# Router weights spread over the rows by DMA instead of by matmuls, in a gated cross-attention and mixture-of-experts block

## The reference, cut to what matters

```python
x = x + tanh(g_xattn) * xattn(layernorm(x), ctx)      # (4, 256, 256): both sides rounded to fp8 blocks, then x @ ctx.T
x = x + tanh(g_ffn) * ffn(layernorm(x))
def ffn(x):                                           # 1024 tokens of 256; 8 experts of 176 rows, top 4; shared of 704
    probs = softmax(x @ gate_w.T)
    comb = top4(probs), divided by their sum, 0 elsewhere         # (tokens, 8)
    y_e = (silu(x @ wg_e.T) * (x @ wu_e.T)) @ wd_e.T
    sh = (silu(x @ swg.T) * (x @ swu.T)) @ swd.T
    return sum_e comb_e * y_e + sigmoid(x @ shared_gate_w.T) * sh
```

## Time and profile before

| | us |
|---|---|
| median of 3 runs (lowest to highest) | 190.42 (189.87 to 191.33) |
| the profiled execution, its own time | 189.87 |
| its span | 188.1 |
| TensorE busy | 163.8 (87%) |
| VectorE busy | 127.6 (68%) |
| ScalarE busy | 103.8 (55%) |
| GpSimd busy | 90.8 (48%) |

### The profile page before, as it was taken

How to read it: one execution, slowest core, us unless ns; L and a number is a source line. 1 busy time by engine, 2 the same in 40 slices (tenths; PEclk the granted TensorE clock), 3 DMA queues, 4 the chain that set the end, 5 groups by cost and what they waited for, 6 DMA issues and landing times.

```text
span 188.1 us, 2346 instructions
## 1 busy us (share of the span) xinstructions
PE 163.8 (87%) x747; PEld 124.8 (66%) x755; DVE 127.6 (68%) x273; ACT 103.8 (55%) x231; POOL 90.8 (48%) x95
## 2 busy tenths in 40 slices
PE   0122798999959999999999999999999999999993
PEld 0010357878737777777777787887777777777761
DVE  1888974989997779998965424988347544544453
ACT  2499462976528986547485564445754444444330
POOL 6120612664543254847668426544645555856310
PEclk9999999999999999999999999999999999999999
DMA  4999991000000000000000000200000000000002
GB/s 140 271 375 356 334 348 49 2 0 0 0 0 3 0 0 2 2 0 3 0 0 2 0 3 0 112 0 0 0 0 0 3 2 0 0 0 3 0 0 112
DMA packets 4368, 9.97 MB, mean 53 GB/s; under 512 B 617, under 2 KB 617, under 8 KB 4356
## 3 DMA queue, kind: packets, MB, share of 16 engines
q1 hardware_dynamic: 4356, 9.83, 15.3%
HBM read 8.78 MB, written 1.05 MB: 52 GB/s over the span
## 4 chain that ended last, share of the span: by engine, by line
PE 71%; DVE 16%; ACT 7%; issue 2%; DMA 2%; DVEq 0%
PE bank L943 62%; DVE a_lo L736 3%; PE bank L901 2%; PE bank L996 2%; DVE act L725 2%; DMA x<-xs 2%; ACT xc L360 1%; PE bank L982 1%; ACT cw L352 1%; DVE comb_parts L714 1%; DVE x L643 1%; PE bank L987 1%; PE bank L983 1%; DVE up L698 1%; ACT xc L343 1%
## 5 line engine op out<-in xcount | busy, mean ns | idle before, releaser
L296 POOL TENSOR_TENSOR gu_lo<-w_raw,gu_hi 128x512 fp32r<-128x512 f32 (+1 forms) x34 | 49.2, 1447 | 26.6 <-ACT gu_hi L426 18.6
L943 PE MATMUL bank<-h_hi,gu_hi 128*128 128x512 f32 x124 | 52.8, 425 | 0.0
L303 POOL TENSOR_TENSOR d_lo<-w_raw,d_hi 128x256 fp32r<-128x256 f32 (+1 forms) x34 | 27.3, 804 | 49.3 <-ACT d_hi L431 49.2
L725 DVE TENSOR_TENSOR act<-silu,bank 128x512 f32<-128x512 f32 (+1 forms) x34 | 23.3, 686 | 40.3 <-PE bank L943 37.7
L440 ACT ACTIVATE silu<-bank 128x512 f32<-128x512 f32 (+1 forms) x34 | 20.3, 596 | 51.9 <-PE bank L943 50.3
L943 PE MATMUL bank<-h_hi,gu_lo 128*128 128x512 f32 x124 | 48.5, 391 | 0.0
L943 PE MATMUL bank<-h_lo,gu_hi 128*128 128x512 f32 x124 | 48.3, 389 | 0.0
L943 PE MATMUL bank<-a_hi,d_hi 128*128 128x512 f32 (+1 forms) x68 | 28.5, 419 | 0.5 <-DVE a_lo L736 0.4
L736 DVE TENSOR_TENSOR a_lo<-act,a_hi 128x512 fp32r<-128x512 f32 (+1 forms) x34 | 26.1, 768 | 1.1 <-ACT a_hi L448 0.7
L943 PEld LDWEIGHTS bank<-h_hi,gu_lo 128*128 128x128 f32 x124 | 23.3, 188 | 5.3
L943 PE MATMUL bank<-a_hi,d_lo 128*128 128x512 f32 (+1 forms) x68 | 26.7, 392 | 0.0
(11 more groups left out here) (117 smaller groups left out, 185.1 us busy)
## 6 DMA issues: line engine op xcount, KB each, us to landing
w_raw<-w_full SPq DMA_DIRECT2D x16, 384.0 KB, 4.7
x<-xs SPq DMA_DIRECT2D x4, 256.0 KB, 6.8
cw<-ctx_t SPq DMA_DIRECT2D x4, 256.0 KB, 6.0
out_t<-fin SPq DMA_DIRECT2D x4, 256.0 KB, 2.1
w_raw<-w_last SPq DMA_DIRECT2D x1, 256.0 KB, 6.8
spread<-sel SPq DMA_DIRECT2D x1, 111.4 KB
small_in<-small SPq DMA_DIRECT2D x1, 11.0 KB, 6.4
```

The source lines that it names most:

```text
L296: nc.gpsimd.tensor_tensor(gu_lo[:, slot, 0:cols], w_raw[:, c, 0:cols], gu_hi[:, slot, 0:cols].bitcast(F32), ALU.subtract).then_inc(gu_lo_d ...
L303: nc.gpsimd.tensor_tensor(d_lo[0:rows, slot, :], w_raw[0:rows, c, at:at + D], d_hi[0:rows, slot, :].bitcast(F32), ALU.subtract).then_inc(d ...
L725: nc.vector.tensor_tensor(act[0:rows, slot, :], silu[0:rows, slot, :], up, ALU.mult).then_inc(gated_done, 1)
L943: last = nc.tensor.matmul(out, w[k][a], x_of[k][b], start=(start and k == 0 and i == 0), stop=(stop and k == blocks - 1 and i == 2))
```

## The change

It does the following.

- The router weights, in float32, are turned to rows of experts (9 x 512, four transposes), copied to SBUF, and written by a DMA to a scratch array in DRAM. SP waits for it and issues 19 DMAs, each reading one row of 512 and writing it to as many partitions as that expert has in a chunk: 18 for the 11 chunks and one for the shared weight. `mix`, `mix_shared`, `copy_sg`, `route_split`, `spread` and its load go. `mixed` reads the tile `mixw` in SBUF.
- From the third expert unit of a half on, `mixed` comes before `gated`: it multiplies the silu by the weight, and `gated` multiplies that by the up product.
- The router's high and low gate weights are stacked in one tile, so that `router` takes 4 matmuls, and DVE adds the two parts when it reads the logits.
- The small unit's down weights are stored twice, and its high and low activations are stacked on 128 partitions, so that its down product takes 4 matmuls instead of 6.
- Gate and up weight parts have three slots (`SPLIT`) instead of two. `high_gu` and `low_gu` run two units ahead instead of one.
- `route_compare`, `route_rank`, `route_weigh` of the first half and `transpose_comb` of both are moved one unit earlier; work on batches 2 and 3 is moved by up to two units, mostly later, and uses other banks.
- The last down product starts before its low part is there (`down_last`).

```diff
+SPLIT = 3
+def weighs_silu(n):
+    return n % UNITS >= SHARED_UNITS + 2
+def owners(c):
+    first, last = c * P // EI, ((c + 1) * P - 1) // EI
+    return [(e, max(e * EI - c * P, 0), min((e + 1) * EI - c * P, P)) for e in range(first, last + 1)]
...
-        gu_hi = sb("gu_hi", [P, 2, GU], F32R)
-        gu_lo = sb("gu_lo", [P, 2, GU], F32R)
+        comb_rows = sb("comb_rows", [G, HN])
+        mixw = sb("mixw", [P, EXPERT_UNITS + 1, HN])
+        gu_hi = sb("gu_hi", [P, SPLIT, GU], F32R)
+        gu_lo = sb("gu_lo", [P, SPLIT, GU], F32R)
...
@@ sync @@
-            sp.wait_ge(spread_zeroed, 1)
-            sp.dma_start(spread[0:3 * G, 0:ROWS], sel).then_inc(sel_landed, 16)
...
+            def spread_comb(h):
+                sp.wait_ge(comb_ready, h + 1)
+                sp.dma_start(comb_d[h], comb_rows[:]).then_inc(comb_out, 16)
+                sp.wait_ge(comb_out, 16 * (h + 1))
+                if h >= 1:
+                    sp.wait_ge(mixed_done, h * EXPERT_UNITS)
+                    sp.wait_ge(shared_taken, h * KC)
+                for c in range(EXPERT_UNITS):
+                    for e, lo, hi in owners(c):
+                        sp.dma_start(mixw[lo:hi, c, :], comb_d[h, e:e + 1, :].to_broadcast((hi - lo, HN)))\
+                            .then_inc(mixw_landed[c], 16)
+                    if c == 1:
+                        sp.dma_start(sg, comb_d[h, E:E + 1, :].to_broadcast((P, HN))).then_inc(sg_landed, 16)
+            spread_comb(0)
+            store(0, 0)
+            store(0, 1)
+            spread_comb(1)
...
@@ gpsimd @@
             low_d(0)
+            low_gu(2)
             for n in range(1, ALL):
-                if n + 1 < ALL:
-                    low_gu(n + 1)
+                if n + 2 < ALL:
+                    low_gu(n + 2)
...
@@ scalar @@
             for n in range(ALL):
-                if 1 <= n < ALL - 1:
-                    high_gu(n + 1)
-                if n == 6:
+                if n < ALL - 2:
+                    high_gu(n + 2)
+                if n == 5:
                     copy_comb(0)
...
                 silu_unit(n)
...
@@ vector @@
+                by_part = LOGIT_T[:, 0:HT * 2 * GP].rearrange("p (j i g) -> p j i g", j=HT, i=2)
+                after(did(nc.vector.tensor_reduce(lg[:], by_part.rearrange("p j i g -> p j g i"), op=ALU.add, axis=AX.X)))
...
             def mixed(n):
-                v.wait_ge(mix_done, mixes(n) + 1)
-                nc.vector.tensor_tensor(act[:, slot, :], act[:, slot, :], MIX[:], ALU.mult).then_inc(mixed_done, 1)
+                v.wait_ge(mixw_landed[c], 16 * len(owners(c)) * (n // UNITS + 1))
+                factor = silu if weighs_silu(n) else act
+                nc.vector.tensor_tensor(act[:, slot, :], factor[:, slot, :], mixw[:, c, :], ALU.mult).then_inc(mixed_done, 1)
...
             for n in range(ALL):
+                if weighs_silu(n):
+                    mixed(n)
+                    low_a(n - 1)
                 gated(n)
-                if n >= 1:
+                if n >= 1 and not weighs_silu(n):
                     low_a(n - 1)
                 if n == 1:
+                    routed = route_compare(0)
+                if n == 2:
                     max_x_2 = max_x(2)
                     scales_x(2, max_x_2)
+                    ranked = route_rank(routed)
+                if n == 3:
+                    route_weigh(0, ranked)
...
@@ tensor @@
                 if h >= 1:
-                    pe.wait_ge(mixed_done, h * EXPERT_UNITS)
-                three_passes(LOGIT[:], [(gate_hi[:, k, :], gate_lo[:, k, :]) for k in range(KC)], tokens(h), True, True)
+                    pe.wait_ge(comb_ready, h)
+                for k, parts in enumerate(tokens(h)):
+                    for i, part in enumerate(parts):
+                        last = nc.tensor.matmul(LOGIT[:], gate_w[:, k, :], part, ...)
...
             def transpose_comb(h):
-                pe.wait_ge(comb_split, h + 1)
+                pe.wait_ge(comb_done, h + 1)
                 for jj in range(HT):
-                    last = nc.tensor.transpose(view[:, jj * P:(jj + 1) * P], comb_parts[:, jj, :], eye_b[:])
+                    last = nc.tensor.transpose(COMBT[0:G, jj * P:(jj + 1) * P], comb[:, jj, :], eye[:])
...
+                    if is_small(n):
+                        nc.tensor.matmul(out[k][:], d_hi[0:2 * LAST, slot, ks], a_hi[0:2 * LAST, slot, :], start=False, stop=False)
+                        last = nc.tensor.matmul(out[k][:], d_lo[0:rows, slot, ks], a_hi[0:rows, slot, :], start=False, stop=True)
...
+            def down_last():
+                pe.wait_ge(d_lo_done, n + 1)
+                pe.wait_ge(a_hi_done, n + 1)
...
                 gate(n)
+                if n == 2:
+                    transpose_logits(0)
                 if not is_small(n):
                     up(n)
...
-                if n == UNITS + 6:
-                    mix_shared(1)
-                if n == ALL - 1:
-                    mix(n)
                 down(n - LAG)
-                if n % UNITS == SHARED_UNITS - 1:
+                if n % UNITS == SHARED_UNITS - 2:
                     transpose_comb(n // UNITS)
-                if is_expert(n) and n < ALL - 1:
-                    mix(n)
             down(ALL - 2)
-            down(ALL - 1)
+            down_last()
```

More of the change, by code:

```diff
@@ L22 @@
 EXPERT_UNITS = E * EI // P
-assert E * EI % P == 0
+assert E * EI % P == 0 and 2 * LAST == P
 SHARED_UNITS = UNITS - EXPERT_UNITS
@@ L143, in flamingo_gated_block @@
         a_lo = sb("a_lo", [P, DEEP, HN], F32R)
-        sg = sb("sg", [P, HN])
+        sg = mixw[:, EXPERT_UNITS, :]
         shared = sb("shared", [P, KC, HN])
@@ L404, in copy_logits @@
                 a.wait_ge(logits_ready, h + 1)
-                nc.scalar.activation(lg_rows[:], LOGIT[0:GP, :], ACT.Copy).then_inc(logits_copied, 1)
+                nc.scalar.activation(lg_rows[:], LOGIT[0:2 * GP, :], ACT.Copy).then_inc(logits_copied, 1)
             def tanh_router(h):
@@ L412, in copy_comb @@
                 a.wait_ge(comb_psum, h + 1)
-                nc.scalar.activation(comb_t[:, h], combt_view(h), ACT.Copy).then_inc(comb_ready, 1)
-            def copy_sg(h):
-                a.wait_ge(mix_done, mixes(h * UNITS + SHARED_UNITS))
-                nc.scalar.activation(sg[:], MIX[:], ACT.Copy).then_inc(sg_copied, 1)
+                nc.scalar.activation(comb_rows[:], COMBT[0:G, :], ACT.Copy).then_inc(comb_ready, 1)
             def high_gu(n):
-                c, slot = CHUNKS[n % UNITS], n % 2
+                c, slot = CHUNKS[n % UNITS], n % SPLIT
                 cols = GUL if is_small(n) else GU
@@ L430, in high_d @@
                 at = GUL if is_small(n) else GU
+                rows = 2 * LAST if is_small(n) else rows
                 nc.scalar.activation(d_hi[0:rows, slot, :], w_raw[0:rows, c, at:at + D], ACT.Copy).then_inc(d_hi_done, 1)
@@ L443, in high_a @@
                 slot, rows = n % DEEP, rows_of(n)
-                if is_expert(n):
+                if is_expert(n) and not weighs_silu(n):
                     a.wait_ge(mixed_done, experts(n) + 1)
@@ L853, in _ @@
                     take_shared(n // UNITS, 1)
-                if is_expert(n):
+                if is_expert(n) and not weighs_silu(n):
                     mixed(n)
+                if n == 13:
+                    residual_sum(3)
             low_a(ALL - 1)
@@ L920, in router @@
                 if h >= 1:
-                    pe.wait_ge(mixed_done, h * EXPERT_UNITS)
-                three_passes(LOGIT[:], [(gate_hi[:, k, :], gate_lo[:, k, :]) for k in range(KC)], tokens(h),
-                             True, True).then_inc(logits_ready, 1)
+                    pe.wait_ge(comb_ready, h)
+                for k, parts in enumerate(tokens(h)):
+                    for i, part in enumerate(parts):
+                        last = nc.tensor.matmul(LOGIT[:], gate_w[:, k, :], part, start=(k == 0 and i == 0),
+                                                stop=(k == KC - 1 and i == 1))
+                last.then_inc(logits_ready, 1)
             def transpose_logits(h):
@@ L1020, in down @@
                     ks = slice(k * P, (k + 1) * P)
-                    last = three_passes(out[k][:], [(d_hi[0:rows, slot, ks], d_lo[0:rows, slot, ks])],
-                                        [(a_hi[0:rows, slot, :], a_lo[0:rows, slot, :])], start, stop)
+                    if is_small(n):
+                        nc.tensor.matmul(out[k][:], d_hi[0:2 * LAST, slot, ks], a_hi[0:2 * LAST, slot, :], start=False, stop=False)
+                        last = nc.tensor.matmul(out[k][:], d_lo[0:rows, slot, ks], a_hi[0:rows, slot, :], start=False, stop=True)
+                    else:
+                        last = three_passes(out[k][:], [(d_hi[:, slot, ks], d_lo[:, slot, ks])],
+                                            [(a_hi[:, slot, :], a_lo[:, slot, :])], start, stop)
                     if stop:
```

(12 more changed lines are left out.)

231 lines of the change are left out of this document (99 added, 132 removed).

## The result

The changed kernel takes 185.81 us (median of 4 runs, 185.49 to 186.05) against 190.63 for the kernel before in the same comparison: a ratio of 0.974, 95% interval 0.970 to 0.978. Faster, as forecast, but by 4.8 us where 9.6 had been summed, and the time lies 0.6 above the upper end of the range.

The account below looks back on a forecast made before the run. PE was taken as the bound from 31 us on: slots times start distance, plus waits. Terms 6.7 + 1.8 - 0.4 + 2.2 + 0.5 = 10.8, less 1.2, gave 9.6: 190.42 - 9.6 = 180.8 us, range 178.6 to 185.2.

Parts of the forecast that it names:

- Mixes, 6.7: PE's list: removing 22 mixes and one `mix_shared` per half, 24 at 0.28 us each, gains 6.7 us.
- What is left keeps its length: PE from 31 us on: time is slots times start distance, so removed instructions save their full distance; no size given.
- the opposite case: Whole kernel: an end before 178 us would mean matmuls cost less without the mixes; not counted on.
- Router and small unit, 1.8: Both halves: each router and each small down product loses 2 of 6 matmuls, 8 at 0.227 us, gaining 1.8 us.
- Comb transposes, -0.4: Both halves: four float32 transposes take 0.44 us against 0.24 with bf16 input, a loss of 0.4 us.
- The wait before the transposes, 2.2: First half, before the comb transposes: PE's 2.4 us wait shrinks to 0.2, gaining 2.2 us.
- second rival: First half: router work on DVE meets POOL, the wait before the comb transposes stays, 183.0 us; chance 0.12.
- The end, 0.5: Last down product: one DVE instruction leaves the path and the low part is needed later, gaining 0.5 us.
- DMAs at nothing: Weight write and broadcasts replacing the mixes: landing taken as 2.1 us, hidden under 6 us of cover, cost 0.
- Three slots at nothing: Gate and up weight parts: PE never waited for one, so a third slot gives nothing by itself, priced 0.
- What DVE pays, 1.2: Units 6 to 16: POOL blocks 11 more two-SBUF-input DVE instructions, 0 to 6.4 us; 1.2 us loss taken.
- first rival: Units 6 to 16: DVE and POOL become the bound and blocking reaches PE, 184.5 us; chance 0.22.

Follow-up runs that it names:

- dummy mixes: Changed kernel with one unused bf16 matmul (128x128 weights, 512 columns) behind each of 11 second-half expert units; 188.18 us, ratio 0.984.
- the late broadcasts: Changed kernel with SP waiting for the silu of the first expert unit before it issues the broadcasts; 186.27 us, ratio 0.975.
- their experiment: Changed kernel with `stats_x1(3)` on DVE at the end of unit 13 instead of unit 14; 184.81 us, ratio 0.967.
- six blocks in the kernel's order: Changed kernel plus 32-byte pad, with 27 matmul blocks behind it at varied byte offsets; these six alternate high and low parts; 284.73 us with all blocks.
- block at (64,0): In that same 284.73 us run, a block of 15 equal matmuls, weights offset 64 bytes, columns 0; it took 3.58 us.

## Why the prediction was wrong

By its own steps, in the order of the sum:

- **Mixes, 6.7: right.** The dummy mixes cost 0.25 each on the same base. With the place mended, an expert unit takes 4.08 instead of 4.355, 0.275 less.
- **What is left keeps its length: wrong, and it was no term at all.** Matmuls went from 0.2267 to 0.2322. Over 30 units of the profiles (from the start of unit 3 to that of unit 33), the changed kernel against the one with 160 bytes more, 133.06 against 130.91 us: **2.2**; the medians differ by 1.9. The second has 0.5 us more of waits in these units, so the matmuls alone are some 2.6. Shown: the start of the tiles does it, in both kernels and in both directions. In the kernel before, where units have a mix, it cost less (0.8 and 1.4 us, the second with a lower clock in part). The prediction priced the instructions that the change removes, adds and moves; that removing and adding tiles moves all tiles behind them was not looked at. In the prediction's last part I had named only the opposite case, matmuls that get shorter.
- **Router and small unit, 1.8: wrong by 1.6.** The small down product lost 2 of 6 matmuls, priced at 0.227 each, but its remaining 4 come 0.43 apart: 1.7 us for 1.36. The failed step is the price of 0.227 for a matmul taken out of six of one form, where the rows of those that stay change from one to the next.
- **Comb transposes, -0.4: right**, four float32 took 0.37 here (49.58 to 49.95), which makes 0.3 of it.
- **The wait before the transposes, 2.2: short by 1.4.** 0.90 was left, not 0.2, and 0.73 for `diag` came right behind it. That it is a tie was right, that the work keeps its length was not: from the read of the logits to the weights it took 12.6 us (36.93 to 49.53) and not 11.2, since two instructions of 0.2 took 0.78 and 0.75 beside POOL. That was bad luck, by some nanoseconds of one start: two other traces had it the other way, and no wait there. The second rival named this; its price (2.2) was too high: 1.6 of waits stood there against the 0.2 forecast, 1.4 more.
- **The end, 0.5: right.** The last down product starts 0.23 after the matmul before it, and not 0.76.
- **DMAs at nothing: right**, by the late broadcasts. The size was off (landing 5.4 us, not 2.1; from the write's issue to the first broadcast's 1.5 us, not 2.2), and the 6 us of cover held it.
- **Three slots at nothing: wrong as a reason, right in the sum.** Of itself the slot gives nothing over before, but without it and the lead of two units the rest of the change loses 4.3 us. "PE never waited for a weight part" was read in a kernel whose DVE had 21% to spare.
- **What DVE pays, 1.2: right in size.** DVE was busy 46.0 us, within 41.05 to 47.5, and the waits of units 15 and 16 were 0.93 (1.39 by their experiment). These rows answer to the earlier trace rows (DVE's groups from 53.1 to 104.5 us: busy, mean ns, idle before):

```profile
L753 DVE TENSOR_TENSOR a_lo<-act,a_hi 128x512 fp32r<-128x512 f32 x11 | 12.4, 1129 | 0.0
L747 DVE TENSOR_TENSOR act<-silu,mixw 128x512 f32<-128x512 f32 x9 | 8.4, 936 | 3.4 <-ACT silu L457 3.3
L747 DVE TENSOR_TENSOR act<-act,mixw 128x512 f32<-128x512 f32 x2 | 2.5, 1230 | 0.0
```

All three have two SBUF inputs and ran 0.25 to 0.55 us over the 0.68 of an unblocked one. That is as the rule of the Trainium skill that the prediction weighed has it ("SBUF — State Buffer", section "Who interferes with whom"). The 9.0 us of idle time before `gated` have shrunk to 3.4 + 0.9. The blocking is there in full; the idle time took nearly all of it, so the first rival (DVE as the bound, 184.5) did not come about, though the time came out near its figure. A time that fits a rival does not show its cause.

The account against 9.6: place 2.2, small unit 1.6, waits at 49 and 52 us 1.4, less 0.3 (waits of units 15 and 16 smaller than the 1.2 allowed) makes 4.9 of the 5.2 that are missing. It closes so well by some luck. The place alone is nearer 2.6, and unit 3 began at 39.82 us where it had begun at 40.75, which is 0.9 earlier and 0.5 more than the router's two matmuls account for. With both set right, 5.3 stand against 5.7, and 0.4 stay open. With both size errors mended and the statistics earlier, 181.24 was measured, 0.4 above the 180.8 that were forecast. The 0.4 is that small because two errors cancel: without the 1.2 that were allowed and with 1.67 of waits at 50 and 53 us in place of 0.2, the forecast would have been 181.1.

## What to carry to other kernels

When PE is full, its time is count times distance, and the distance is a measurement too: print where the matmul's tiles begin before and after a change, and watch the spacing of an untouched unit before looking for waits. A removed matmul is worth its distance only if its neighbours keep their shape. A schedule that puts two engines' instructions on the same moment will be measured with the wait and without it, so look at the starts before giving a small difference a cause. And before calling a buffer or a lead superfluous, ask whether the rest of the change takes away the idle time that made it so.

## What was new about the hardware

- float32r matmuls (128x128 weights, 512 columns) come 0.2267 us apart when weights and columns begin at the same place modulo 256 bytes, and 0.232 to 0.234 otherwise (gate and up products 1.39 to 1.40 us for six, where they took 1.36). The six blocks in the kernel's order had, from their second matmul on, 229.2 to 229.6 ns against 232.3 to 233.6. Open are why the blocks differ by 3 to 4 ns and the kernel's gate and up products by 5 to 7, why the first three matmuls of the down product share in it, why units with a mix feel it less (0.04 us and not 0.10), and the block at (64,0).
- Matmuls with weights of 128 and 64 rows in turn come 0.43 us apart, with the weight load 0.24 to 0.25 late; with 128 rows in all, 0.23.
- A DVE instruction with two SBUF inputs of 32 columns took 0.77 to 0.78 us when a POOL instruction had begun 7 to 19 ns before it, and 0.19 when POOL had begun 1 to 4 ns before it.
- The broadcasts (12 tiles of 256 KB a half, in 19 DMAs issued back to back, each source row 2 KB of DRAM) land in 3.4 to 6.1 us; the queues moved 251 to 272 GB/s in the fullest slices.
- PE stood for 3.51 us up to 98.02. The granted clock was 0.63 in the stretch from 96 to 100 us and 0.52 in the next 4 us, then 1.00. A wait of 2.26 us (kernel before with 128 bytes more) was followed by 0.84 and 0.73, one of 2.25 (kernel before) by 1.00. Of 13 executions of the kernel before, 8 had a mean granted clock of 0.988 to 0.991 and took 190.8 to 191.5 us, the other 5 had 0.997 to 1.000 and took 189.8 to 190.4; that its wait is the reason is not shown.
